# A block of cross-attention and a quantized feed-forward layer: key and query splits moved ahead of the roundings on GpSimd, and a maxima product moved between the score pairs of TensorE's job-free steps

## The reference, cut to what matters

```python
x = x + xattn(layernorm(x), ctx, ctx)        # q, k, v, o projections with biases, softmax over 1601 keys, 16 heads
x = x + ffn(layernorm(x))

def fp4_quant_dequant(x):                    # blocks of 16 along the last dimension
    scale = max(max(abs(xb)) / 6.0, 1e-12)
    q = GRID[searchsorted(MID, abs(xb / scale))] * sign(xb) * scale
def fp4_linear(x, w): return einsum(fp4_quant_dequant(x), fp4_quant_dequant(w))
ffn(x) = fp4_linear(silu(fp4_linear(x, w_gate)) * fp4_linear(x, w_up), w_down)
```

## Time and profile before

| | before |
|---|---|
| median of 3 runs | 1806.91 us (1804.79 to 1809.01) |
| profiled execution, its own time | 1806.17 us |
| its span in the trace | 1804.4 us |
| TensorE busy | 1666.5 us (92%) |
| VectorE busy | 1422.4 us (79%) |
| ScalarE busy | 1131.0 us (63%) |
| GpSimd busy | 562.2 us (31%) |

### The profile page before, as it was taken

How to read it: one execution, slowest core, us unless ns; L and a number is a source line. 1 busy time by engine, 2 the same in 40 slices (tenths; PEclk the granted TensorE clock), 3 DMA queues, 4 the chain that set the end, 5 groups by cost and what they waited for, 6 DMA issues and landing times.

```text
span 1804.4 us, 26956 instructions
## 1 busy us (share of the span) xinstructions
PE 1666.5 (92%) x9408; PEld 660.9 (37%) x9408; DVE 1422.4 (79%) x2077; ACT 1131.0 (63%) x2293; POOL 562.2 (31%) x673
## 2 busy tenths in 40 slices
PE   5798889999998999989999999989999899989958
PEld 2332234334432344333443334423343334323325
DVE  5778888878786887969788788878879697798447
ACT  2366667666676667666676666766677666666731
POOL 4327530532126220343205421162202532012204
PEclk8899999999998999999999999999999999999979
DMA  6644332232324313252331423243132422300000
GB/s 157 145 77 124 71 74 43 67 95 51 61 43 115 79 39 59 48 123 52 63 55 50 106 57 61 43 106 81 38 57 57 93 46 49 57 7 10 13 21 12
DMA packets 106482, 117.51 MB, mean 65 GB/s; under 512 B 23140, under 2 KB 87660, under 8 KB 106348
## 3 DMA queue, kind: packets, MB, share of 16 engines
q1 hardware_dynamic: 101808, 111.93, 29.3%
q10 hardware_dynamic: 4540, 3.87, 0.9%
HBM read 76.78 MB, written 30.16 MB: 59 GB/s over the span
## 4 chain that ended last, share of the span: by engine, by line
PE 77%; DVE 10%; ACT 5%; issue 4%; POOL 1%; DMA 0%; SPq 0%; ACTq 0%; POOLq 0%; DVEq 0%
PE pvb L824 20%; PE st L795 19%; PE mx L809 10%; PE misc L725 7%; PE misc L697 5%; DVE cmx L1051 4%; PE misc L690 4%; ACT prob L976 3%; PE misc L745 3%; PE misc L737 2%; PE misc L676 2%; PE misc L711 1%; PE misc L733 1%; PE misc L766 1%; DVE ht L1080 1%
## 5 line engine op out<-in xcount | busy, mean ns | idle before, releaser
L976 ACT ACTIVATE prob<-st 128x512 f32<-128x512 f32 (+1 forms) x1584 | 863.7, 599 | 385.3 <-PE st L795 382.8
L1051 DVE TENSOR_REDUCE cmx<-mx 128x2 f32<-128x1024 f32 x768 | 905.7, 1219 | 216.1 <-PE mx L809 212.8
L795 PE MATMUL st<-qstack,kstack 112*128 112x512 bf16 (+1 forms) x1584 | 500.0, 389 | 53.8 <-ACT prob L976 44.0
L824 PE MATMUL pvb<-prob,vv 128*32 128x512 f32 (+1 forms) x3328 | 446.9, 609 | 0.6 <-ACT prob L976 0.6
L795 PEld LDWEIGHTS st<-qstack,kstack 112*128 112x128 bf16 (+1 forms) x1584 | 128.6, 99 | 516.3 <-issue 247.0
L809 PE MATMUL mx<-kstack,qstack 48*128 48x512 bf16 (+1 forms) x2048 | 255.6, 339 | 29.5 <-DVE cmx L1051 16.4
L1306 POOL TENSOR_TENSOR ht<-ht,rh 128x352 f32<-128x352 f32 (+1 forms) x78 | 57.3, 759 | 462.2 <-DVE rh L1027 462.2
L725 PE MATMUL misc<-wguT,rowsT 128*128 128x352 f32 x456 | 154.3, 460 | 0.0
L1298 POOL TENSOR_TENSOR ht<-ht,mt 128x352 f32<-128x352 f32 (+1 forms) x140 | 124.6, 913 | 74.1 <-DVE mt L1208 60.7
L809 PEld LDWEIGHTS mx<-kstack,qstack 48*128 48x128 bf16 x2048 | 58.2, 94 | 203.4 <-issue 134.3
L1312 POOL TENSOR_TENSOR cin<-cin 128x400 f32<-128x400 f32 (+1 forms) x60 | 58.3, 972 | 233.2 <-ACT cin L916 233.2
(11 more groups left out here) (182 smaller groups left out, 1556.7 us busy)
## 6 DMA issues: line engine op xcount, KB each, us to landing
kstack<-scr_k SPq DMA_DIRECT2D x384, 100.1 KB, 4.3
scr_k<-cin SPq DMA_DIRECT2D x48, 300.0 KB, 3.9
qstack<-scr_q SPq DMA_DIRECT2D x372, 32.0 KB, 1.8
cin<-ctx_in SPq DMA_DIRECT2D x16, 512.0 KB, 5.3
scr_q<-qp SPq DMA_DIRECT2D x16, 384.0 KB, 4.5
scr_k<-cin SPq DMA_DIRECT2D x16, 300.8 KB, 4.9
xn<-x SPq DMA_DIRECT2D x8, 512.0 KB, 4.0
cin<-ctx_in SPq DMA_DIRECT2D x16, 256.0 KB, 5.5
```

The costliest lines, as they stand in the source:

```text
L795: mm(score_bank(it, n, h)[0:KROWS[kt], :], kstack[:, hd, KOFF[kt]:KOFF[kt] + KROWS[kt]], qstack[:, hd, :], start=True, stop=True).then_inc ...
L824: last = mm(pvb[2 * D * h:2 * D * (h + 1), :], vv[0:w, kt, (HG * g + h) // 2, D * (h % 2):D * (h % 2 + 2)], prob[0:w, n % 2, h, :], start= ...
L976: activate(prob[0:KROWS[kt], n % 2, 2 * pair + h, :], score_bank(it, n, 2 * pair + h)[0:KROWS[kt], :], ACT.Exp, scale=SCALE).then_inc(exp_ ...
L1051: v.tensor_reduce(cmx[:, g % 2, h0:h0 + 2, at:at + 1], products, op=ALU.max, axis=AX.X).then_inc(max_free, 1)
```

## The change

Two edits. First, in `POOL_WORK`: before, GpSimd's order from step 11 on was k1, q0, xround 0, k2, k3, k4, xround 1, q1, k5, k6, k7. Now it is k1, q0, k2, k3, xround 0, k4, q1, xround 1, k5, k6, k7. Only the six loop iterations have both the splits (early) and the roundings (late), so in "first" and "last" the order on GpSimd stays as it was.

Second, on TensorE: in a job-free step with scores, the first of the two maxima products is issued between the two score pairs, and the second behind the second pair. Before, both stood behind it. This touches the 30 job-free steps of "first" and "last" that carry maxima.

```diff
 POOL_WORK = {
-    0: [("late", "bias", 0)], 10: [("early", "k", 0)], 11: [("early", "k", 1)], 12: [("early", "q", 0)], 13: [("late", "xround", 0), ("early", "k", 2)],
-    14: [("early", "k", 3)], 15: [("early", "k", 4)], 16: [("late", "xround", 1), ("early", "q", 1)], 17: [("early", "k", 5)], 18: [("early", "k", 6)], 19: [("early", "k", 7)],
+    0: [("late", "bias", 0)], 10: [("early", "k", 0)], 11: [("early", "k", 1)], 12: [("early", "q", 0), ("early", "k", 2)], 13: [("early", "k", 3)],
+    14: [("late", "xround", 0), ("early", "k", 4)], 16: [("early", "q", 1), ("late", "xround", 1)], 17: [("early", "k", 5)], 18: [("early", "k", 6)], 19: [("early", "k", 7)],
```

```diff
                     for job in jobs(it, n, 0):
                         shared(job)
+                    products = maxima(it, n)
+
+                    between = 1 if has_att and not jobs(it, n, 0) else 0
+                    for job in products[:between]:
+                        pair_products(job)
                     if has_att:
                         scores(n, 1)
-                    products = maxima(it, n)
-                    for job in products[:2]:
+                    for job in products[between:2]:
                         pair_products(job)
```

## The result

| | before | after |
|---|---|---|
| median | 1807.05 us (4 runs, 1804.79 to 1809.01) | 1757.24 us (4 runs, 1755.79 to 1759.96) |
| ratio to before | | 0.9727, 95% interval 0.971 to 0.9743 |
| profiled execution, its own time | 1806.17 us | 1759.96 us |
| span in the trace | 1804.4 us | 1758.2 us |

The change makes the kernel 2.7% faster. The measured time is 9 us over the forecast of 1748, inside the range of 1738 to 1764, and falls in the band of rival (a).

A forecast was written before the change was run, and what follows sets the result against it. TensorE was taken as the bound, stalled twice a loop iteration by late key splits. Idle time 36.1 plus clock 23.6, less 3.6, gave 56 us; with 2 for the maxima product, 1806.2 became 1748 us, range 1738 to 1764.

The forecast's parts named there:

- rival (a): GpSimd or VectorE becomes late in the stretch: 6 to 15 us, so 1754 to 1763 us; chance 0.25.
- both stalls: ScalarE's reads of k4 and k7 wait for GpSimd's splits in each loop iteration: 3.54 and 3.25 us of chain.
- Rivals (b) to (e): (b) nothing late, 1738 to 1743, 0.14; (c) second stall stays, 1775, 0.07; (d) wrong cause, 1804, 0.02; (e) slower, 1823, 0.02.
- the cost of the low clock: In six 38 us stretches holding the stalls, TensorE time lost at the lower clock: 23.6 us to be regained.
- no margin at k5, 0.3 us, and 0.3 us for step 19: Deduction per loop iteration for k5's split just in time for k7, and ScalarE's work behind k7: 3.6 us in all.
- The control: Iteration "first", same key and query jobs without roundings: k4 to k7 takes 16.1 us against 21.03 in the second loop iteration.
- Step 19: Step behind k7 with two xqT copies and four exponentials, some 3.3 us of ScalarE: 0.3 us an iteration.
- Edit 2: Maxima product between the score pairs: 0.27 us in 8 of 18 steps of "first", 2 us less.

The follow-up runs named there:

- `first_only`: Kernel before the change with only the first rounding moved, behind k2 and k3, TensorE's order as before: 1785.73 us, ratio 0.9882.
- `last_on_pool`: `both_moved` with the scaling back of the first half (xlast 0) on GpSimd behind xround 0 instead of on VectorE: 1765.69 us, ratio 0.9773.
- `both_moved`: Changed kernel with xround 0 one split earlier (behind k2) and xround 1 one split later (behind k5): 1757.33 us, ratio 0.9725.

## Why the prediction was right or wrong

**Right: the cause and both stalls.** L915's nameless wait was `k_split`; it fell from 51.6 to 6.3 us. All stretches have the full clock, and the rounding's wait halved. `first_only` shows the stalls as two, each with its own price. Rivals (b) to (e) are excluded.

**Mis-sized: the cost of the low clock.** The sum had 23.6 us for it, from (1 - clock) x 38 us. The loop iterations gave 47.8 us in all, and TensorE's idle time fell by 38.5 - 10.35 = 28.2 us. That leaves 19.6 us for the clock, 4.0 less; the busy time of the same six iterations says it directly, with 19.4. The formula counts all time at the lower level as if TensorE's rate had set the pace in it; where it would have waited in any case, the lower rate costs less. That is an argument and no run tests it; the granted clock in the rows, with its two digits, leaves about 1 us either way besides.

**Mis-sized: what is late next.** The step "no margin at k5, 0.3 us, and 0.3 us for step 19" gave 3.6 us; 7.9 us of idle time are left. It failed on VectorE. I had taken `xpower` 0 at 548.26 and `xpower` 1 at 559.8 with the lengths that they had beside an idle GpSimd. The control could not show this: from k4 to k7 "first" has VectorE busy for 10.8 of 18 us, the changed kernel in the second loop iteration for 18.3 of 19, so that "nothing else is late at this pace" was read where VectorE had little to do. In the changed kernel `xpower` 1 ends at 555.7, some 11.4 us after TensorE's k4 (whose read on ScalarE starts at 544.40), where I had 9.2. Its own wait on GpSimd's splits, and the one at step 14, are rival (a), which I priced at 6 to 15 us; it came to 4.3 us over the prediction's 3.6, under the small end of that price. The total lies in the rival's band only because the clock term was off as well, which was luck. The prediction said that VectorE had 34 us of work in 36 us; it should have added what GpSimd's instructions beside it do to that. With the two mis-sized terms, 4.0 + 4.3, 1748 becomes 1756, and the rest is within the spread of the start.

**Step 19** cost next to nothing. **Edit 2** was put at 2 us; the runs allow nothing to 5, so that term is neither confirmed nor refuted.

## What to carry to other kernels

A piece of work that waits for a late producer does not only delay its own consumer: look at what is queued behind it on its engine, and put everything whose inputs are ready in front. When a stall goes, the engine that used to idle beside a busy one starts to work beside it, so take the lengths of the neighbour's instructions from rows where both are busy, not from rows where one waits, and take a control only from a stretch where every engine carries the same work. And once five orders give one length, stop reordering and take work away from the engine that they share, on paper first: it shows in one run whether a bound is an engine or an order.

## What the runs showed of the hardware

A VectorE instruction of 512 columns from and to SBUF (L1169) takes 0.43 us with GpSimd idle and 0.95 to 1.27 us with GpSimd busy; the reductions L1055 of the maxima products, which read PSUM, take 1.20 to 1.23 us each in both cases, all 768 of them in the changed kernel. Moving about one microsecond an iteration from VectorE to GpSimd cost some 8 us in all (`last_on_pool`, 0.9773, against `both_moved`, 0.9725), where a gain of 2 to 5 was expected. In the trace most of that is the clock, next: the iterations without a fall of the clock take 204.0 us, only 0.2 more than in `both_moved`.

The granted TensorE clock fell to its lower level after two pauses of 0.81 and 0.74 us with two matmuls between them, in the second loop iteration of `last_on_pool` (granted clock 0.57 from 557 to 561 us, 1.00 on either side); but not each time. In the third iteration the same two pauses, 0.82 and 0.74 us, left it where it was. Stretches of 12 us around the pair of pauses in the six loop iterations (length, busy time of TensorE and the other engines, then the granted clock):

```profile
346.00:358.00 12.00, 10.44 (x49) 3.42 (x41) 9.76 (x9) 7.07 (x15) 11.53 (x13) 0.86 0.45 97
552.00:564.00 12.00, 10.45 (x50) 3.33 (x42) 9.79 (x10) 6.99 (x14) 11.53 (x13) 0.86 0.44 93
758.00:770.00 12.00, 10.28 (x54) 3.73 (x52) 10.48 (x9) 8.45 (x18) 11.48 (x13) 1.00 0.48 100
962.00:974.00 12.00, 10.28 (x54) 3.72 (x52) 10.46 (x9) 8.46 (x18) 11.47 (x13) 1.00 0.52 101
1166.00:1178.00 12.00, 10.44 (x47) 3.76 (x44) 9.82 (x9) 6.81 (x14) 11.47 (x13) 0.86 0.46 93
1371.00:1383.00 12.00, 10.36 (x55) 3.59 (x55) 10.86 (x10) 8.45 (x18) 11.52 (x13) 1.00 0.48 97
```

The first, second and fifth iteration have the lower clock for a part, and they take 205.6 to 205.8 us; the third and fourth take 204.0. One such fall costs 1.7 us here. All six iterations have the same two pauses to 0.01 us, so the pauses alone do not decide whether it comes; what does, the trace does not show. In `both_moved` pauses of 0.56 and 0.74 us at the same place, and in the changed kernel pauses of 0.18 and 0.84 us behind k4, left the clock at 1.00 in all six.
